# A deformable convolution whose per-batch loads of positions and weights become one transfer each, with the 29th pair of row views copied on chip by Pool

## The reference

```python
def _L0_conv_ref(X, beta):              # whitening with a 16 x 16 matrix
    ...
    for _ in range(T):                  # T = 10
        P = 1.5 * P - 0.5 * (P @ P @ P @ Sigma_N)
    ...
def _dcn_bn_act_res(x, w_off, b_off, w, b, gamma, beta):
    om = conv(x, w_off, padding 1) + b_off          # 27 channels
    off_y, off_x, mask = om[:, :9], om[:, 9:18], sigmoid(om[:, 18:])
    py = off_y + row + ky;  px = off_x + column + kx
    sampled = bilinear(x, py, px) * mask            # per tap, 0 outside the image
    out = einsum('bckhw,ock->bohw', sampled, w) + b
    ...                                              # batch norm
    return jax.nn.relu(out) + x
```

## Time and profile before

| | us |
|---|---|
| median of 3 runs (lowest, highest) | 2781.42 (2772.18, 2787.36) |
| the profiled execution | 2780.72 |
| its span, first to last instruction | 2778.9 |
| PE busy, DVE busy, ACT busy | 1631.9, 1556.4, 1454.1 |
| mean granted clock of PE, share of full speed | 0.795 |
| bytes moved by DMA | 362.34 MB, 130 GB/s over the span |

### The profile page before, as it was taken

The page is one execution under the profiler, slowest core; times in us unless marked ns, Lnnn a source line. Parts: engine busy times, 40 slices in busy tenths (PEclk is TensorE's granted clock), DMA queues, the critical chain, the costliest instruction groups (busy, mean ns, idle before and its releaser), DMA issues. The chain is left out here.

```text
span 2778.9 us, 66692 instructions
## 1 busy us (share of the span) xinstructions
PE 1631.9 (59%) x24206; PEld 1106.2 (40%) x24207; DVE 1556.4 (56%) x1718; ACT 1454.1 (52%) x2219; POOL 24.0 (1%) x17
## 2 busy tenths in 40 slices
PE   5559900000058866868668686786776867876340
PEld 5433300000046545545445454554554645554120
DVE  5250055455157756767557575575766756876214
ACT  2112233323058756767557676675766856875001
POOL 1000000000100000000000000000000000000000
PEclk9689955555569988889889898898988988998555
DMA  2377855675877868668676686676866867772006
GB/s 97 83 192 216 221 160 171 185 229 162 199 117 133 133 99 138 114 106 137 98 115 118 109 140 101 103 132 105 140 102 110 137 106 121 133 123 43 3 0 284
DMA packets 197854, 362.34 MB, mean 130 GB/s; under 512 B 87600, under 2 KB 175975, under 8 KB 181737
## 3 DMA queue, kind: packets, MB, share of 16 engines
q1 hardware_dynamic: 136852, 286.47, 53.9%
q10 hardware_dynamic: 60758, 72.05, 8.3%
HBM read 253.93 MB, written 104.46 MB: 129 GB/s over the span
## 5 line engine op out<-in xcount | busy, mean ns | idle before, releaser
L945 DVE TENSOR_TENSOR G<-odd_y,ps_odd_v 128x1008 f32<-128x1008 f32 (+2 forms) x464 | 541.8, 1168 | 547.2 <-PE ps_odd_v L822 547.1
L805 PE MATMUL ps_odd_y<-rows,sel 32*128 32x504 f32 (+1 forms) x896 | 468.2, 523 | 576.3 <-DMA rows<-scratch_parts 417.9
L822 PE MATMUL ps_even_v<-tent_x,stage 32*128 32x171 f32 (+2 forms) x5568 | 592.4, 337 | 238.1 <-issue 220.7
L901 ACT COPY even_v<-ps_even_v 128x1008 f32<-128x1008 f32 (+2 forms) x464 | 450.7, 971 | 457.7 <-PE ps_odd_v L822 456.6
L822 PE MATMUL ps_odd_v<-tent_x,stage 32*128 32x171 f32 (+3 forms) x5568 | 603.7, 331 | 34.6 <-issue 34.5
L895 ACT COPY odd_y<-ps_odd_y 128x504 f32<-128x504 f32 (+2 forms) x928 | 526.3, 567 | 98.5 <-PE ps_odd_y L805 95.7
L822 PEld LDWEIGHTS ps_even_v<-tent_x,stage 32*128 32x128 f32 x5568 | 474.4, 200 | 246.1 <-issue 227.4
L953 DVE TENSOR_TENSOR G<-even_v,ps_even_y 128x1008 f32<-128x1008 f32 (+2 forms) x464 | 538.5, 1161 | 16.8 <-PE ps_even_y L796 14.5
L840 PE MATMUL ps_r<-G,conv_w 128*32 128x224 f32 (+1 forms) x8832 | 515.6, 363 | 5.5 <-issue 4.8
L822 PEld LDWEIGHTS ps_odd_v<-tent_x,stage 32*128 32x128 f32 x5568 | 480.3, 200 | 43.6 <-issue 43.6
L805 PEld LDWEIGHTS ps_odd_y<-rows,sel 32*128 32x128 f32 x896 | 175.6, 196 | 759.4 <-issue 462.1
(11 more groups left out here) (139 smaller groups left out, 897.1 us busy)
## 6 DMA issues: line engine op xcount, KB each, us to landing
place<-scratch_px SPq DMA_DIRECT2D x256, 441.0 KB, 7.0
rows<-scratch_parts SPq DMA_DIRECT2D x256, 220.5 KB, 11.0
scratch_parts<-parts ACTq DMA_DIRECT2D x9, 3136.0 KB, 12.2
scratch_parts<-parts ACTq DMA_DIRECT2D x9, 2688.0 KB, 19.6
x<-scratch_xh SPq DMA_DIRECT2D x48, 406.0 KB, 6.0
scratch_om<-om ACTq DMA_DIRECT2D x64, 196.0 KB, 7.0
scratch_conv<-res SPq DMA_DIRECT2D x448, 14.0 KB, 3.2
image<-scratch_xh SPq DMA_DIRECT2D x4, 1682.0 KB, 25.2
```

The source lines that it names most:

```text
L805: nc.tensor.matmul(ps_odd_y[:, lo:hi], sel[32 * g:32 * g + 32, :], taps(rows, 32 * g, 32, p, lo, hi), start=True, stop=True).then_inc(odd_ ...
L822: m = nc.tensor.matmul(sub(ps_v[g // 2], 0, 128, i * 512 + lo + first, dims), stage[32 * g:32 * g + 32, j * IMAGE + v * C:j * IMAGE + (v + ...
L901: nc.scalar.copy(two(even_v[p % 3], ROW, 2 * p), two(ps_v[0], 512, 2 * p)).then_inc(even_kept, 1)
L945: nc.vector.tensor_tensor(two(G, ROW, v, slot(v)), two(odd_y[p % 3], ROW, v), two(ps_v[1], 512, v), ALU.mult).then_inc(odd_weighted, 1)
```

## The change

Loads: `load_place` is one transfer to 128 partitions, whose source pattern is [4 blocks][the same block 32 times][3528 elements]; `load_rows` is one transfer to the 64 even partitions, source [4 blocks][16 kinds][3528]. So that the four blocks of a pair lie one behind the other, the DRAM layout becomes [quarter][image][parity], the positions stage puts the quarter ahead of the image in its partitions (its loads and range stores have the pattern [4][32][...] in DRAM), and group g is now image g // 2, parity g % 2. The last row of the last quarter goes to slot 0 of the image's first block, where its taps are free, so the zero-filled edges and their eight transfers disappear, and the 29th step's data are in slot 0 of batch 0: Pool copies them to `last_place` and `last_rows` once per pair, and its semaphores let SP overwrite batch 0's buffers.

```diff
-PARITY_STRIDE = (4 * B + 1) * BATCH
-KIND_STRIDE = 2 * PARITY_STRIDE
+BLOCK_STRIDE = 2 * B * BATCH
+KIND_STRIDE = 4 * BLOCK_STRIDE
...
-                base = parity * PARITY_STRIDE + tap * GROUP * W
+                base = parity * BATCH + tap * GROUP * W
                 if (q + ky - parity) // 2 == 0:
-                    return [(base, 0, GROUP)]
-                return [(base + W, 0, GROUP - 1), (base + BATCH, GROUP - 1, 1)]
+                    return [(base, 0, 128, 0, GROUP)]
+                return [(base + W, 0, 128, 0, GROUP - 1), (base + BLOCK_STRIDE, 0, 96, GROUP - 1, 1),
+                        (base, 96, 32, GROUP - 1, 1)]
...
-                                                      [[OM_IMG, B], [DCH, 4], [1, DCH]])).then_inc(loaded[b], 16)
+                                                      [[DCH, 4], [OM_IMG, B], [1, DCH]])).then_inc(loaded[b], 16)
...
-                        sp.dma_start(dram(name, n * H, [[KK * H, B], [RPC, 4], [1, RPC]]),
+                        sp.dma_start(dram(name, n * H, [[RPC, 4], [KK * H, B], [1, RPC]]),
...
                 def load_place(pair, n):
-                    load("px", place, place_loaded, pair, n, [0, 32])
+                    sp.dma_start(place[n % 2][:, :], dram("px", n * BLOCK_STRIDE + pair * 4 * BATCH,
+                                                          [[BATCH, 4], [0, 32], [1, BATCH]])).then_inc(place_loaded[n % 2], 16)
 
                 def load_rows(pair, n):
-                    load("parts", rows, rows_loaded, pair, n, [KIND_STRIDE, Y_KINDS])
+                    pitch = rows[n % 2][:].ap[0][0]
+                    sp.dma_start(bass.AP(tensor=rows[n % 2][:].tensor, offset=0, ap=[[2 * pitch, 64], [1, BATCH]]).bitcast(fp32),
+                                 dram("parts", n * BLOCK_STRIDE + pair * 4 * BATCH,
+                                      [[BATCH, 4], [KIND_STRIDE, Y_KINDS], [1, BATCH]])).then_inc(rows_loaded[n % 2], 16)
...
-                                sp.wait_ge(distant, STEPS * it + GROUP * (n + 1))
+                                if n == 0:
+                                    sp.wait_ge(place_read, it + 1)
+                                else:
+                                    sp.wait_ge(distant, STEPS * it + GROUP * (n + 1))
...
-                        if p == GROUP:
-                            load_place(it, BATCHES - 1)
-                            load_rows(it, BATCHES - 1)
...
+                def body(it, last):
+                    wait(pool, distant, STEPS * it)
+                    pool.wait_ge(place_loaded[0], 16 * (2 * it + 1))
+                    pool.tensor_tensor(turn[:, 0:1], turn[:, 4:5], turn[:, 4:5], ALU.add)
+                    pool.tensor_copy(sub(place[2], 0, 128, 0, [[W, KK], [1, W]]),
+                                     sub(place[0], 0, 128, 0, [[GROUP * W, KK], [1, W]])).then_inc(place_loaded[2], 1)
+                    wait(pool, even_spread, STEPS * it)
+                    pool.wait_ge(rows_loaded[0], 16 * (2 * it + 1))
...
+                    pool.wait_ge(distant, STEPS * it + GROUP)
+                    pool.wait_ge(place_loaded[2], it + 1)
+                    pool.tensor_tensor(turn[:, 2:3], turn[:, 4:5], turn[:, 4:5], ALU.add).then_inc(place_read, 1)
...
```

More of the change, by code:

```diff
@@ L501, in program @@
             ranges = [sb(n, KK * RPC) for n in RANGES]
[L502 removed]
+            grid_loaded = sem("grid_loaded")
             loaded = [sem(f"loaded{i}") for i in range(2)]
@@ L540, in _ @@
                 sp.dma_start(column[:, :], dram("column", 0, [[W, 128], [1, W]])).then_inc(grid_loaded, 16)
[L541 to L545, removed]
                 for n in range(KK):
@@ L589, in store @@
                     for q in range(2):
-                        for to, row, count in runs(n, q):
-                            act.dma_start(dram("parts", to, [[BATCH, 128], [KIND_STRIDE, Y_KINDS], [1, count * W]]),
-                                          sub(parts[b], 0, 128, q * HALF + row * W, [[DCH, Y_KINDS], [1, count * W]]).bitcast(fp32)
+                        for to, part, npart, row, count in runs(n, q):
+                            act.dma_start(dram("parts", to, [[2 * BATCH, npart], [KIND_STRIDE, Y_KINDS], [1, count * W]]),
+                                          sub(parts[b], part, npart, q * HALF + row * W, [[DCH, Y_KINDS], [1, count * W]]).bitcast(fp32)
                                           ).then_inc(stored[b], 16)
@@ L649, in program @@
             G = sb("G", G_SLOTS * 2 * ROW)
+            turn = sb("turn", 5, parts=1)
             res = sb("res", UPX)
@@ L686, in taps, with arrived @@
                 return sub(tile[BUFFERS[n]], part, parts, lo // W * pitch + p % GROUP * W, [[pitch, (hi - lo) // W], [1, W]])
-            def times(n, it):
-                return it + 1 if BUFFERS[n] == 2 else 2 * it + n // 2 + 1
+            def arrived(loaded, n, it):
+                if n == BATCHES - 1:
+                    return loaded[2], it + 1
+                return loaded[n % 2], 16 * (2 * it + n // 2 + 1)
             def slot(v):
@@ L778, in _ @@
                     pool.memset(tile, 0.0).then_inc(cleared, 1)
+                pool.memset(turn[:, :], 0.0).then_inc(cleared, 1)
+                pool.wait_ge(cleared, 5)
+                def body(it, last):
[6 more added lines that the diff above has]
+                    pool.wait_ge(rows_loaded[0], 16 * (2 * it + 1))
+                    pool.tensor_tensor(turn[:, 1:2], turn[:, 4:5], turn[:, 4:5], ALU.add)
+                    pool.tensor_copy(sub(rows[2], 0, 128, 0, [[W, KK], [1, W]]),
+                                     sub(rows[0], 0, 128, 0, [[GROUP * W, KK], [1, W]]).bitcast(fp32)).then_inc(rows_loaded[2], 1)
+                    pool.wait_ge(distant, STEPS * it + GROUP)
+                    pool.wait_ge(place_loaded[2], it + 1)
+                    pool.tensor_tensor(turn[:, 2:3], turn[:, 4:5], turn[:, 4:5], ALU.add).then_inc(place_read, 1)
+                    pool.wait_ge(even_spread, STEPS * it + GROUP)
+                    pool.wait_ge(rows_loaded[2], it + 1)
+                    pool.tensor_tensor(turn[:, 3:4], turn[:, 4:5], turn[:, 4:5], ALU.add).then_inc(rows_read, 1)
+                peel(pool, PAIRS, body)
             @block.tensor
@@ L787, in rows_ready @@
                     if p % GROUP == 0:
-                        n = p // GROUP
-                        pe.wait_ge(rows_loaded[BUFFERS[n]], 16 * 4 * times(n, it))
+                        pe.wait_ge(*arrived(rows_loaded, p // GROUP, it))
                 def spread_even(it, p):
@@ L795, in spread_even @@
                     for i in range(2):
-                        m = nc.tensor.matmul(ps_even_y[:, i * 512 + lo:i * 512 + hi], sel[32 * i:32 * i + 32, :],
-                                             taps(rows, 32 * i, 32, p, lo, hi), start=True, stop=True)
+                        m = nc.tensor.matmul(ps_even_y[:, i * 512 + lo:i * 512 + hi], sel[64 * i:64 * i + 32, :],
+                                             taps(rows, 64 * i, 32, p, lo, hi), start=True, stop=True)
                     m.then_inc(even_spread, 1)
```

41 lines of the change are left out of this document (17 added, 24 removed).

## The result

The changed kernel takes 3567.12 us (median of 4 runs, 3547.7 to 3597.06), the kernel before in the same series 2783.14: a ratio of 1.283, with a 95% interval of 1.273 to 1.294. It is 784 us slower. The forecast was 3135 us, some 352 slower, with 3430 as the upper end of the range: the sign was right, the size was not.

A forecast was written before the change was run, and what follows sets the result against it. It took the sampling stage's PE, ACT, DVE chain plus a loop-jump gap as the bound, with tap loads bounding the positions stage. 2780.7 + 114 (positions) + 16 (start) + 224 (sampling) = 3135 us, range 2880 to 3430.

The forecast's parts named there:

- Four engines: New loads and the positions stage's loads and range stores, slowest count 4, spread over 4 DMA engines; forecast 0.62.
- Rival 2: Transfers still spread over 16 engines, so loads, start and gap get faster; 2730 us, chance 0.09.
- +114: Positions stage: removed edge transfers, loads on four engines and extra issues sum to 114 us more, bounds 80 and 150.
- 0.53 us for 14,112 bytes: Time of one piece on one DMA engine, from 417 GB/s over 16 engines.
- The start term of +16: Start of the sampling stage: first two batches' loads take 50.4 us instead of 33; +16 us, bounds 10 and 20.
- Rival 3: Place is slow because each block is read 32 times, 1.06 us a piece; about 3920 us, chance 0.09.
- The queue becomes the bound: Sampling stage: loads take 26.9 us per batch against 23.7 of compute, bounding three batches; 123.8 us a pair.
- Some 4 us a pair are taken for that: Sampling stage: ACT waits in result for res stores queued behind loads; some 4 us a pair.
- 16 us of gap: Sampling stage: the loop-jump gap plus PE's other issue gaps, about 16 us a pair, kept in the changed pair's time.
- At nothing: Removed 29th-step transfers, Pool's two copies and the extra hop in SP's waits cost nothing; below 1 us a pair otherwise.
- PE, ACT and DVE do the same instructions in other partitions: Compute engines: their work only moves to other partitions, listed among the parts priced at nothing.
- Rival 1: Four engines, but loads run ahead during the gap and PE never waits in the sampling stage; 2911 us, chance 0.13.

The follow-up runs named there:

- blocks_repeated: One transfer of loads_alone, with the pattern of place: four blocks, each read 32 times, to 128 partitions; 32 us.
- rows_alone: One transfer of loads_alone: the same 1.8 MB from 128 rows, one slowest count of 128; 7.1 us.
- split_all: Changed kernel with each load whose slowest count is 4 made into four transfers, in both stages; 2669.78 us, 0.964 of the kernel before.
- split_sampling: Changed kernel with only the sampling stage's loads, place and rows, split by group of 32 partitions; 2730.84 us, 0.986 of the kernel before.
- blocks_distinct: One transfer of loads_alone: 128 different blocks to 128 partitions on four engines; 29.5 to 32.8 us in the later rounds.
- res_seven: Changed kernel with seven res tiles instead of one, each with its own semaphore; 3112.14 us, 1.119 of the kernel before.
- after_jump: split_all with the loads of the next pair's batch 1 held until the first sample after the jump; 2629.91 us, 0.948 of the kernel before.
- rows_adjacent: split_all with the 16 kinds of weights back in 16 adjacent partitions of a group; 2814.24 us, 1.014 of the kernel before.
- loads_alone: A kernel that computes nothing and issues single transfers, each waited for, four times over; its transfers of 14,112-byte pieces were timed one by one.

## Why the prediction was right or wrong

**Four engines: right.** The argument was a count of completion packets for transfers of like counts; the 4 for unlike ones was the author's estimate from it. The DMA share of 0.25 beside a lone `place`, the 32 us and 4 packets under 512 B of `blocks_repeated` against 7.1 us and 16 of `rows_alone`, and the 897 us between the changed kernel and split_all show it for unlike counts. Rival 2 (2730) falls, though its time is near what the layout gives once the count is repaired (split_sampling 2730.84, by another sum).

**Positions stage, "+114": right as a sum,** +115 measured, and ACT's wait for `ox` is 40.65 us where 41 was named. Its terms are not confirmed by that. The sum gave 16.8 + 91 = 108 us to the loads on four engines; with these loads on 16 engines again (split_all) the stage gets 77 us shorter, although nine more issues a tap count against it. How much those issues take was not measured, so the close agreement may in part be luck. That reordered loads give 49 us (58 in the kernel before) shows that the wait for them was on the path.

**The price of one engine, "0.53 us for 14,112 bytes": too low where it counts.** The 14,112-byte packets of the changed kernel have a median of 0.535 us but a mean of 0.709, and 0.97 as a mean in the first 13 us behind the issue at 1028.0, when four engines begin `place` together. The step took the rate of 16 engines in a load to 128 partitions, 417 GB/s, and missed that four engines, each filling its own 32 partitions, meet in pairs (31.6 us for partitions 0 to 63, 19.4 for 32 to 95). `place` alone is therefore 30 to 32 us and not 16.8. The start term of +16 became +38 (its own numbers, 50.4 less 33, give 17). Rival 3 gave this observable, over 30 us with no queue ahead, but for a wrong reason: `blocks_distinct` is as slow. Its 3920 is too high because the mean piece is 0.709 us and not 1.06.

**"The queue becomes the bound" of three batches, 123.8 us a pair without the `res` part: about right in size, partly by luck.** res_seven, where nothing else is left, takes 1953.8 / 16 = 122.1 us a pair. It is not the same sum: the piece is dearer (0.605 us as a mean of the run), the gap is smaller, and the queue holds the pair even there.

**"Some 4 us a pair are taken for that": the step that failed.** This was the `res` store behind the load. The prediction named the mechanism, the line and the reason, and set 64 us on it; taking the wait away gave 455 us back, 438 of them in the sampling stage. It should have followed from its own numbers: behind 16.8 us and more of `place`, with 13.6 us to the next block and a wait at every one of four batches, ACT stands still at least 3.2 us (16.8 - 13.6) four times a pair, some 200 us in the run as an estimate, and since ACT's distances set the next `place` free, it is not made up later. The bounds had it only as part of +30 a pair "if every batch waited for res as well". With `place` at 30 us it is four waits a pair of 11.0 us as a mean and 17.0 at most. The larger part, 321 us, shows as dearer pieces beside it: the sum priced the store's delay and the pieces apart, and the runs show them move together.

**"16 us of gap" kept: wrong in the kernel's favour.** PE's issue waits fell from 220.7 to 48.5 us. The idea that instructions come through the same DMA engines stood under rival 2 only, though four busy engines leave twelve free (the changed kernel's page gives the instruction queue 222 packets and 0.4% of the 16 engines' span). after_jump shows that the gap depends on the loads beside it: 77 us less of issue wait for 40 us of time.

**At nothing:** Pool's copies (0.592 us each for `last_place`) and its extra hop held nobody up for long enough to see: rows_adjacent has them, and its sampling stage is 13 us shorter than before. The waits that Pool itself has are idle time off the path. But "PE, ACT and DVE do the same instructions in other partitions" was read as a cost of nothing and so hid a gain: 144 us from `rows` in every second partition. The rate of 113 GB/s for `rows` was in view, and the gain was given to rival 2 alone.

**Rival 1** (2911, loads hidden) falls with the pair at 150 us.

## What to carry to other kernels

Folding several transfers into one can change on how many DMA engines it runs. Here a slowest count of 16, 32 or 128 used them all (16 packets under 512 B a transfer in loads_alone), and a 4 on one side left four of 16 (4 packets): the issues saved cost three quarters of the engines, 32 us for 1.8 MB that took 7.1 us on 16. Then ask what small, single-buffered transfer is issued behind the big one on the same queue, and price it at the big one's whole time less the time until it is waited for, once for every such wait. And look where rows land in SBUF and what is in the queues when a loop jumps: 16 rows in every second partition, and loads held back until after the jump, were worth 144 and 40 us here without any work less.

## What the hardware did that was not expected

- Engines of one transfer delay each other by where they write: 31.6 us for 64 partitions from 0, 19.4 us for 64 from 32, of the same bytes and source. Four engines with 64 even partitions take 12.4 to 15.4 us, with a mean piece of 0.68 us; why not 0.53 stayed open.
- Alone, 16 rows of 14 KB take 3.6 us in adjacent and 3.3 us in even partitions, nearly the same; in the kernel, with all groups in the queue, the difference is 144 us of time and 10.9 against 8.1 us of landing. The measurement alone would have dismissed it.
- The stall at the loop's jump depends on the traffic: 12.83 us with the loads of before, 9.73 with those of split_all, 4.00 in the changed kernel and 3.53 in after_jump, for the same 222 instruction packets. The DMA share in these gaps is 0.89, 0.88, 0.44 and 0.29; since the first two are alike, the share alone does not set the length. In the kernel before, two packets of the instruction queue fall in the gap, between 1093.2 and 1106.0 us; that the engines wait for them is inferred. The wait is longer with loads in the queues; what exactly it stands behind is not shown.
